# Four scans from kept last states, the third tile added by GpSimd in every step, and membrane and group statistics read from PSUM

## The reference, cut to what matters

```
xn = groupnorm(x)                          # 32 groups of 8 channels
xh, z = split(xn @ W_in)                   # 512 + 512 channels
xc = depthwise_conv_3x3(xh)
dt_r, B, C = split(xc @ W_xproj)           # 8, 16, 16
dt = softplus(dt_r @ W_dt + b_dt)
dtN = dt @ W_dtN + b_dtN
for t in range(2304):                      # per image, 512 channels d, 16 states n
    h[d,n] = exp(dt[t,d] * A[n]) * h[d,n] + dtN[t,n] * B[t,n] * xc[t,d]
    y[t,d] = sum_n h[d,n] * C[t,n] + Dskip[d] * xc[t,d]
x = x + (layernorm(y) * ln_g + ln_b) * silu(z) @ W_out + b_out

u = groupnorm(x) @ W.T + b                 # the 8 images are the 8 time steps
for t in range(8):
    v = v + (u[t] - v) / 2                 # membrane, one value for each pixel and channel
    s = v >= 1
    v = v * (1 - s)
    x[t] = x[t] + s
```

## Time and profile before

| | us |
|---|---|
| median of 3 runs | 4882.54 |
| the runs | 4874.4, 4884.55, 4882.54 |
| the profiled execution | 4875.24 |
| its span in the profile | 4873.4 |
| DVE, POOL, PE, ACT busy | 4382.4, 4151.5, 3694.4, 3122.2 |

### The profile page before, as it was taken

The page is one execution under the profiler, slowest core; times in us unless marked ns, Lnnn a source line. Parts: engine busy times, 40 slices in busy tenths (PEclk is TensorE's granted clock), DMA queues, the critical chain, the costliest instruction groups (busy, mean ns, idle before and its releaser), DMA issues.

```text
span 4873.4 us, 75732 instructions
## 1 busy us (share of the span) xinstructions
PE 3694.4 (76%) x20244; PEld 2332.2 (48%) x20244; DVE 4382.4 (90%) x4205; ACT 3122.2 (64%) x4578; POOL 4151.5 (85%) x3243
## 2 busy tenths in 40 slices
PE   4788787778777777777877777777777777877766
PEld 1455444545454544455544544445544554544443
DVE  0899999999999999999999999899989999999994
ACT  1677676666766676666766666666666666666662
POOL 1899999888988899888988889888888888998891
PEclk8889888988988899888888889998988898889986
DMA  2222212222222212222222212222221222122200
GB/s 56 85 65 74 66 58 65 77 69 63 62 69 67 76 47 78 60 77 60 65 63 73 64 57 78 67 60 60 80 71 50 60 84 67 59 63 70 68 32 20
DMA packets 189421, 315.36 MB, mean 65 GB/s; under 512 B 51992, under 2 KB 164120, under 8 KB 188960
## 3 DMA queue, kind: packets, MB, share of 16 engines
q1 hardware_dynamic: 188960, 310.06, 21.6%
HBM read 171.87 MB, written 20.05 MB: 39 GB/s over the span
## 4 chain that ended last, share of the span: by engine, by line
issue 30%; POOL 30%; DVE 18%; PE 15%; ACT 2%; SPq 2%; DVEq 1%; POOLq 1%; DMA 1%; ACTq 0%
POOL st L543 24%; DVE st L955 11%; PE ht L1088 5%; DVE y L932 3%; PE work L1061 2%; PE work L1154 2%; SPq L416 2%; POOL y L590 2%; POOL carry L567 1%; POOL st L550 1%; POOL xb L599 1%; PE work L1161 1%; PE work L1115 1%; PE work L1148 1%; PE work L1173 1%
## 5 line engine op out<-in xcount | busy, mean ns | idle before, releaser
L955 DVE TENSOR_TENSOR_SCAN st<-decay,st 128x1024 f32<-128x1024 f32 (+1 forms) x1536 | 2729.0, 1777 | 123.2 <-ACT decay L696 47.8
L543 POOL TENSOR_TENSOR st<-xc,bbc 128x1536 f32<-128x1536 f32 x768 | 2649.6, 3450 | 14.0 <-DMA bbc<-brow 11.1
L696 ACT ACTIVATE decay<-dt,neg_a 128x1024 f32<-128x1024 f32 (+1 forms) x1536 | 1360.1, 900 | 640.9 <-DVE st L955 634.3
L1088 PE MATMUL ht<-ident,st 128*128 128x128 f32 x9216 | 1414.2, 309 | 384.4 <-DVE st L955 382.2
L1088 PEld LDWEIGHTS ht<-ident,st 128*128 128x128 f32 x9216 | 1205.4, 159 | 683.9 <-issue 435.9
L932 DVE SCALAR_TENSOR_TENSOR y<-ht,ct,y 128x512 f32<-128x512 f32 x1536 | 1117.7, 728 | 129.2 <-PE ht L1088 126.6
L590 POOL TENSOR_TENSOR y<-y,weighed 128x512 f32<-128x512 f32 x624 | 792.6, 1270 | 276.0 <-ACT weighed L717 273.5
L717 ACT ACTIVATE weighed<-ht,ct 128x512 f32<-128x512 f32 x624 | 427.5, 685 | 438.6 <-PE ht L1088 436.0
L1061 PE MATMUL work<-tri,conv_w 96*32 96x384 f32 x4608 | 485.8, 561 | 130.6 <-issue 82.7
L1120 PE MATMUL work<-xn,win 128*128 128x384 f32 x768 | 318.6, 556 | 119.6 <-DVE ob L897 64.9
L1115 PE MATMUL work<-xn,win 128*128 128x480 f32 x768 | 359.2, 592 | 5.1 <-ACT xn L813 3.1
(11 more groups left out here) (93 smaller groups left out, 3870.8 us busy)
## 6 DMA issues: line engine op xcount, KB each, us to landing
bbc<-brow SPq DMA_DIRECT2D x192, 768.0 KB, 4.7
tri<-xhp SPq DMA_DIRECT2D x2304, 50.0 KB, 2.0
xin<-in_x_dram SPq DMA_DIRECT2D x48, 384.0 KB, 3.2
out_dram<-ot SPq DMA_DIRECT2D x48, 384.0 KB, 5.6
brow<-xp SPq DMA_DIRECT2D x48, 24.0 KB, 1.5
win<-in_L_conv_W_in_dram SPq DMA_DIRECT2D x1, 1024.0 KB
wo<-in_L_conv_W_out_dram SPq DMA_DIRECT2D x1, 512.0 KB
w1s<-in_L_conv_W_dram SPq DMA_DIRECT2D x1, 256.0 KB, 3.3
```

The costliest lines, as they stand in the source:

```text
L543: u = g.tensor_tensor(slot, xc[:, kq % 2, :, :], bbc[:, piece_slot(kq, p), n % PIECE, :].unsqueeze(1).to_broadcast([P, DC, T]), ALU.mult)
L696: a.activation(flat(decay[:, :, :])[:, lo:hi], flat(dt[:, (k + ahead) % 2, :, :])[:, lo:hi], ACT.Exp, scale=neg_a[:, n:n + 1]).then_inc(s_ ...
L955: v.tensor_tensor_scan(state[:, lo:hi], flat(decay[:, :, :])[:, lo:hi], state[:, lo:hi], 0.0 if h == 0 else state[:, lo - 1:lo], ALU.mult, ...
L1088: last = t.transpose(ht[:, m, c * P:(c + 1) * P], st[:, j, c, m * P:(m + 1) * P], ident[:, :])
```

## The change

It has these parts.

1. Scans: four for each step, one for each channel group of 384 columns. Each starts from the last state that is kept in `carry` (from the constant 0 in iteration 0). The first column's 1e30, `a0`, `cs`, POOL's small additions and the waits for them are gone. The last states are now copied by ACT, right after the decays of the next step (`save_carry`). The decays keep their two parts; scans 0 to 2 of a step come before the first addition to y, scan 3 before the second; scan 2 waits for the second decay part as well.
2. OWN is gone: ACT weighs and POOL adds the third tile in all 16 steps.
3. Membrane: DVE charges in place in PSUM (`charge_and_fire`: work + bias + volt, then the comparison with the threshold plus the image), for each half in its own step, between scan 3 and the second addition to y. ACT copies the charge from PSUM to `volt`, after its carry copy (`copy_membrane`). At the end of the step DVE resets from PSUM and the copy (`reset`), and only this frees the bank. So that the factor 0.5 needs no instruction, volt is kept in a unit that doubles from image to image (`units`, `b1cs`, and a factor in `w1s`).
4. Group statistics: the deviation from the mean and its square are read from and written to the PSUM bank, so that no instruction has two SBUF tensors; the bank is freed at the end.

```diff
-OWN = (8, 10, 11,)
-NWT = NS - len(OWN)
 CUT = 1024
-FAR = 1e30
-LEAST = 1e-28
+PARTS = ((0, CUT), (CUT, DC * T))
...
             def scan_input(b, k, n, ahead):
...
-                u = g.tensor_tensor(slot, xc[:, kq % 2, :, :],
-                                    bbc[:, piece_slot(kq, p), n % PIECE, :].unsqueeze(1).to_broadcast([P, DC, T]),
-                                    ALU.mult)
-                if kq > 0:
-                    u.then_inc(s_ux, 1)
-                    pool.wait_ge(s_ux, (bq * (K - 1) + kq - 1) * NS + n + 1)
-                    pool.wait_ge(s_cs, (bq * (K - 1) + kq - 1) * NCS + 1 + max(0, n - NCOPY + 1))
-                    g.tensor_tensor(st[:, j, :, 0], st[:, j, :, 0], cs[:, :, n], ALU.add).then_inc(s_u, 1)
-                else:
-                    u.then_inc(s_u, 1)
+                g.tensor_tensor(st[:, j, :, :], xc[:, kq % 2, :, :],
+                                bbc[:, piece_slot(kq, p), n % PIECE, :].unsqueeze(1).to_broadcast([P, DC, T]),
+                                ALU.mult).then_inc(s_u, 1)
...
             def accumulate_last(b, k, n, before):
...
-                if n in OWN:
-                    return
...
+                def save_carry(n, before):
+
+                    kq = (k - before) % K
+                    i = (b * K + k - before) * NS + n
+                    act.wait_ge(s_scan, i + 1)
+                    a.activation(carry[:, :, n], st[:, (kq * NS + n) % 3, :, T - 1], ACT.Copy).then_inc(s_carry, 1)
...
+                def copy_membrane(kc, h):
+
+                    act.wait_ge(s_spike, ((b - 1) * K + kc) * CH + h + 1)
+                    hold("act", act, b)
+                    i = turn(b, k, f"l{kc}_{h}")[0]
+                    a.activation(volt[:, h, kc * T:(kc + 1) * T], work[:, i, 0:T], ACT.Copy).then_inc(s_kept, 1)
...
                     next_decay(s)
+                    if main and k < K - 1:
+                        save_carry(s, 0)
+                    for kc, a0_step in (L1_SLOTS.get(k, ()) if L1 in do else ()):
+                        if s in (a0_step, a0_step + 1):
+                            copy_membrane(kc, s - a0_step)
...
-                v.tensor_copy(gn_mu[w][:, :], work[:, i, 0:CH]).then_inc(emptied[i], 1)
...
+                mean, off, square = (work[:, i, j * CH:(j + 1) * CH] for j in range(3))
+                v.tensor_copy(gn_mu[w][:, :], mean)
+                v.tensor_tensor(gn_dm[w][:, :], gn_mv[w][:, :, 0], mean, ALU.subtract).then_inc(s_gdv[w], 1)
+                v.tensor_tensor(off, gn_mv[w][:, :, 0], mean, ALU.subtract).then_inc(s_gdv[w], 1)
...
-                v.scalar_tensor_tensor(out=volt[:, :, cols], in0=ob[:, :, :], scalar=0.5,
-                                       in1=volt[:, :, cols], op0=ALU.mult, op1=ALU.add).then_inc(s_volt, 1)
...
+                now = work[:, i, 0:T]
+                v.scalar_tensor_tensor(out=now, in0=now, scalar=b1s[:, h:h + 1], in1=volt[:, h, cols],
+                                       op0=ALU.add, op1=ALU.add).then_inc(s_volt, 1)
+                dve.wait_ge(s_volt, il + 1)
+                hold("dve", dve, b)
+                v.scalar_tensor_tensor(out=ob[:, h, :], in0=now, scalar=units[:, 1:2],
+                                       in1=img[:, img_par(b, -1), h, cols], op0=ALU.is_ge,
+                                       op1=ALU.add).then_inc(s_spike, 1)
+
+            def reset(b, k, kc, h):
...
+                dve.wait_ge(s_kept, ((b - 1) * K + kc) * CH + h + 1)
+                hold("dve", dve, b)
+                i = turn(b, k, f"l{kc}_{h}")[0]
+                now = work[:, i, 0:T]
+                v.scalar_tensor_tensor(out=volt[:, h, cols], in0=now, scalar=units[:, 1:2], in1=volt[:, h, cols],
+                                       op0=ALU.is_lt, op1=ALU.mult).then_inc(emptied[i], 1)
...
-            def scan(b, k, n, h):
+            def scan(b, k, n, c):
...
+                if c == 0:
                     dve.wait_ge(s_u, i + 1)
+                    if k > 0:
+                        dve.wait_ge(s_carry, (b * (K - 1) + k - 1) * NS + n + 1)
+                    dve.wait_ge(s_dec[0], i + 1)
+                if c == 2:
+                    dve.wait_ge(s_dec[1], i + 1)
+                state = st[:, (k * NS + n) % 3, c, :]
+                last = v.tensor_tensor_scan(state, decay[:, c, :], state, carry[:, c, n:n + 1] if k > 0 else 0.0,
+                                            ALU.mult, ALU.add)
+                if c >= 2:
+                    last.then_inc((s_scan0, s_scan)[c - 2], 1)
```

More of the change, by code:

```diff
@@ L339, in flat @@
             return v.rearrange("p c t -> p (c t)")
-        def weighings(q, n):
-            return q * NWT + sum(m not in OWN for m in range(n))
         def img_par(b, d=0):
@@ L588, in accumulate_last @@
                     pool.wait_ge(s_y2, i)
-                pool.wait_ge(s_wt, weighings(b * K + k - before, n + 1))
+                pool.wait_ge(s_wt, i + 1)
                 g.tensor_tensor(y[:, kq % 2, NTD, :], y[:, kq % 2, NTD, :], weighed[:, n % 2, :],
@@ L718, in weigh @@
                                  scale=ct[:, kq % 2, NTD * NS + n:NTD * NS + n + 1]).then_inc(s_wt, 1)
-                def first_decay():
-                    e = b * (K - 1) + k
-                    act.wait_ge(s_dt, q1 + 1)
-                    need(act, s_cs, e * NCS)
-                    if isinstance(b, int) and b <= 0:
-                        act.wait_ge(s_set_dve, 3)
-                    for c in range(DC):
-                        last = a.activation(a0[:, c, :], neg_a[:, :], ACT.Exp, scale=dt[:, p1, c, 0:1])
-                    last.then_inc(s_a0, 1)
                 def exp_and_log():
@@ L896, in half_charge @@
                 i = await_filled(dve, b, k, f"l{kc}_{h}")
-                v.scalar_tensor_tensor(out=ob[:, h, :], in0=work[:, i, 0:T], scalar=b1s[:, h:h + 1],
-                                       in1=volt[:, h, cols], op0=ALU.add, op1=ALU.subtract).then_inc(emptied[i], 1)
-            def charge(b, k, kc):
-                cols = slice(kc * T, (kc + 1) * T)
-                for h in range(CH):
-                    await_emptied(dve, b, k, f"l{kc}_{h}")
-                v.scalar_tensor_tensor(out=volt[:, :, cols], in0=ob[:, :, :], scalar=0.5,
-                                       in1=volt[:, :, cols], op0=ALU.mult, op1=ALU.add).then_inc(s_volt, 1)
@@ L967, in iteration @@
                         if main:
-                            scan(b, k, s, h)
+                            for c in ((0, 1, 2), (3,))[h]:
+                                scan(b, k, s, c)
+                        if h == 1 and L1 in do:
+                            for kc, a in L1_SLOTS.get(k, ()):
+                                if s in (a, a + 1):
+                                    charge_and_fire(b, k, kc, s - a)
                         if s >= Y_LAG and main:
@@ L1007, in iteration @@
                             if s in (a, a + 1):
-                                half_charge(b, k, kc, s - a)
-                            if s == a + 1:
-                                charge(b, k, kc)
-                            if s == a + 2:
-                                fire(b, k, kc)
+                                reset(b, k, kc, s - a)
                     if TIN in do and k in TIN_CHUNKS and s - 1 in TIN_STEPS:
@@ L1035, in iteration @@
                             jw = await_filled(dve, b, k, "b1")
-                            v.tensor_tensor(b1s[:, :], work[:, jw, 0:CH], b1c[:, :], ALU.add).then_inc(emptied[jw], 1)
+                            dve.wait_ge(s_w1s, b)
+                            v.scalar_tensor_tensor(out=b1s[:, :], in0=work[:, jw, 0:CH], scalar=units[:, 0:1],
+                                                   in1=b1cs[:, :], op0=ALU.mult, op1=ALU.add).then_inc(emptied[jw], 1)
             walk(dve, iteration)
@@ L1081, in transposes @@
                         else:
[L1082 to L1086 removed]
+                            need(pe, s_wt, i)
                         for c in range(DC):
```

123 lines of the change are left out of this document (26 added, 97 removed).

## The result

The changed kernel takes 5010.42 us in the median of 4 runs (4999.72 to 5012.27) against 4881.06 for the kernel before: ratio 1.0262, 95% interval [1.0244, 1.0281], 129 us slower. I had forecast 4950 and slower; the way was right, the rise is not the 70 of that forecast but 129. 5010 lies inside the whole range (4815 to 5030) and just above the 4900 to 5000 of my own case. The profiled executions took 4875.24 and 5012.27, 137 apart; what is read from traces adds up to that, and not to 129.

The account below looks back on a forecast made before the run. POOL was taken to bound steps 8 to 14, DVE steps 14 to 8. +10.7 and -4.4 made +6.3 us an image, +44 for seven; first image +24, tail +2: +70, 4945, stated as 4950; range 4815 to 5030.

Parts of the forecast that it names:

- my own case: The prediction's main case for the whole kernel: 4950 us, 4900 to 5000, chance 0.44.
- the bound it rested on: Steps 8 to 14: POOL is the bound there, busy 32.06 of 33.50 us, and the added additions lengthen them.
- Without a chunk: Steps 8 to 14 without membrane work: +3.1 us, scan 11 starting 1.8 later, at 18.9 after step 8.
- With a chunk at step 9 in iteration 1: Steps 8 to 14: the reset waits for ACT's copy, scan 10 at 13.7, scan 11 at 20.4; +0.9 us.
- The first image: The image without membrane work: 6 x 3.1 us in steps 8 to 14 and some 6 more, +24.
- Iterations 2, 3 and 4 in these steps: Steps 8 to 14: +1.5 us each in iterations 2 and 3 (0.9 to 2.3), +0.6 in 4 (0 to 1).
- Steps 14 to 8: The rest of an image: -4.4 us; -1.4 each in iterations 2 to 4, -2.2 in 1, after 1.7 given back.
- -6.1 + 3.0: Steps 14 to 8, iterations 2 to 4: shorter membrane chunk saves 6.1 us, ten steps with longer scans add 3.0.
- Prices of instructions: DVE: four scans at 0.92 us each (0.87 in the first iteration), new membrane instructions 0.61 (0.53 without overlap).
- ledger -84: DVE's total work: +204 scans, -95 third tile's addition, -160 membrane, -33 group statistics, -84 us.
- The third rival: Scans at the upper bound (+40 us) with iterations 2 and 3 copy stalls at 2.3 (+11): 5000 us, chance 0.12.
- the whole 0.3: DVE's scans: two more a step cost 0.3 us by the row, against 0.12 by the skill's 58 cycles.

Follow-up runs that it names:

- e2: The kernel before with part 2 alone (OWN empty, POOL also adds the third tile for n = 8, 10, 11): 4964.18 us, ratio 1.0152.
- e4: The changed kernel with OWN = (8, 10, 11) back, DVE adding the third tile there, so parts 1, 3 and 4: 4886.1 us, ratio 0.9980.
- e8: The changed kernel with DVE instead of ACT copying the membrane charge in step 9: 4960.66 us, ratio 1.0153, 50 us under the changed kernel.
- e1: The kernel before with parts 3 and 4 alone (membrane and group statistics from PSUM), two scans and OWN kept: 4824.4 us, ratio 0.9874.
- e6: The changed kernel with the third tap's convolution rows left out, 8 DMAs for each channel group instead of 12: 4835.26 us, ratio 0.9888.
- e3: The kernel before with part 1 alone (four scans from kept last states, OWN and old membrane stay): 4978.33 us, ratio 1.0184.

## Why the prediction was right or wrong

**The direction, and the bound it rested on: right.** Steps 8 to 14 cost +14.8 us an image (242.7 against 227.9), and e2 and e4 put all of it on part 2. Without a chunk I had worked out +3.1 us, 36.6 in iteration 5; measured 36.70 there, and 36.39 in iteration 0 (+2.6). Scan 11 at 18.9 us after step 8: 19.0. With a chunk at step 9 in iteration 1, 40.7: 40.89 on the mean, 40.39 in the fourth image, with scan 10 at 13.55 and scan 11 at 20.62 after step 8 (worked out: 13.7 and 20.4). The reset at step 9 waits for ACT as foreseen (e8: 50 us). The first image: +24 forecast, +27.4 measured, but that sum is partly luck: steps 8 to 14 brought 14.1 and not 18.6, the rest 13.3 and not 6.

**Iterations 2, 3 and 4 in these steps: mis-sized.** I bounded 2 and 3 by 0.9 and 2.3 and took 1.5; they cost 2.96 and 2.84, above my upper bound. For iteration 4 I took 0.6; it cost 2.0. Together 4.2 us an image, 25 us in the six images of the table. In iterations 2 and 3 DVE idles 3.05 and 2.9 us in step 9, 1.92 of it before the reset, against 1.9 and 1.65 in iteration 1. Iteration 4 has no chunk at step 9; there scan 11 waits 1.9 us for POOL, as in iterations 0 and 5 (2.2).

**Steps 14 to 8: the step that failed most.** I wrote that the membrane saves 6.1 us in each of iterations 2 to 4 and that "about 1.7 of the gain is given back" to the convolution rows, -4.4 us an image in all. Measured: +1.4 (362.9 against 361.5), 5.8 us an image and 35 in the six images. With the 25 of above this is 60 of the 67 us by which the profiled execution is over the forecast. Iteration 1's stretch fell by 5.7 as against my 2.2; those of 2, 3 and 4 rose by 0.8, 1.1 and 1.8 where I had -1.4.

In e1, without the longer scans, some 24 us less DVE work an image brought 4.8 in the rest. The membrane's saving itself came: DVE's work in the stretch from iteration 1 to 2 fell by 3.25 us (61.26 to 58.01), as -6.1 + 3.0 said. But DVE's idle time in steps 0 to 7 of iterations 2 to 4 rose from 0.5 to 4.8 us, and I had allowed 1.7 for it. e6 shows what it is: with fewer rows that idle time falls to 1.8 and the rest of an image by 19.7.

The traces show why it is so much. Iteration 2 of the fourth image, first the issue of the rows, then the first and the last convolution group; the kernel before:

```profile
2059.95 15.29 SPq L416 DMA_DIRECT2D tri<-xhp  x24
2057.68 2.14 PE L1061 MATMUL work<-tri,conv_w 96*32 96x384 f32 x24
2081.67 2.14 PE L1061 MATMUL work<-tri,conv_w 96*32 96x384 f32 x24
```

The changed kernel:

```profile
2124.23 16.05 SPq L404 DMA_DIRECT2D tri<-xhp  x24
2121.95 2.14 PE L1000 MATMUL work<-tri,conv_w 96*32 96x384 f32 x24
2141.70 3.84 PE L1000 MATMUL work<-tri,conv_w 96*32 96x384 f32 x24 [3.42 <-issue]
```

Counted from scan 0 of the iteration (2043.67 and 2104.31), the first group (cv0, in step 2) went from 14.0 to 17.6. Step 2 now starts at 14.6 and not at 12.1, since DVE's charge, comparison and reset of the first half stand in step 1, and the transposes and the membrane's product still come ahead of cv0 on PE. The last group follows the first by 24.0 us in the kernel before, where nothing holds it, and by 19.8 in the changed kernel, where it waits for the rows; so it comes at 38.0 and 37.4. DVE reached step 6 3.6 us earlier than before and gained nothing by it. I had named this late comer and its place, and priced it from one iteration without a chunk, where DVE's wait is 3.67, without asking when cv0 starts in the iterations that have one.

**Prices of instructions: right.** Scans 0.92 and 0.86 (taken 0.92 and 0.87); membrane 0.60 to 0.62 (taken 0.61); DVE's busy time -105 (ledger -84). The third rival's number (5000) is nearer than mine, but its first half, dearer scans, didn't come; its second, the stalls of iterations 2 and 3, did. The one mechanism of the change that does what it says is the membrane's: L905 took 0.96 to 3.71 us and L913 0.96 to 4.04, while the 288 instructions with one operand in PSUM that came in their place all took 0.60 to 0.63. The traces agree here with the Trainium skill (SBUF — State Buffer, "Who interferes with whom"): with a single SBUF input the instruction no longer waits for GpSimd.

Four scans cost 0.28 us more than two with a kept start value (4 x 0.917 against 2.199 + 1.191 from start to start), and 0.04 more with a constant (4 x 0.857). So a start value from memory costs 0.06; the old second scan had one, the new four have four, which makes 0.18 of the 0.28, and what is left for two more instructions is 0.10. For that part the Trainium skill (VectorE: DVE Perf Modes, "The TRN2 errata", 58 cycles with SBUF operands) gives 0.12, an estimate, and the trace nearly agrees; the page's row for a PSUM source, where the scans' decay lies, has 120 cycles, which would be 0.25, and doesn't fit. In the prediction I set the page's figure against the whole 0.3: I hadn't taken the start values apart.

**How the parts add.** By the medians e1, e2 and e3 make -67, +73 and +87, 93 together, where the changed kernel has +129; by their ratios 103 against 128, and the intervals, of 0.2% to 0.25% each, almost cover the gap. By the table they make -6.7, +9.8 and +12.8 us an image, 15.9 together against 16.3. So on the whole the parts add, as far as these runs can tell. By stretch they don't: in steps 8 to 14 they make -2.0, +14.9 and +16.8 against +14.8, in the rest -4.8, -5.2 and -4.1 against +1.4. That fits the one hold which e6 shows in the rest, the convolution rows: gains that come one by one don't come together. No run tests it. The price of part 2 changes in the same way, 73 us alone and 124 on top of the other parts (by the medians of the changed kernel and e4; 138 by their ratios): 15 us an image in steps 8 to 14 both times, but in the rest e2 gained 5.2 and the changed kernel nothing.

The scans depend on what stands beside them. On top of the new membrane they cost 62 us by the medians of e4 and e1 (52 by their ratios), not 87; in steps 8 to 14, 1.8 us an image (e4 over e1) and not 16.8 (e3 over before). The traces say why, from the distances of DVE's starts in these steps. The scans took 8.3 us more in both. In e4 DVE's idle time fell by 6.2. In e3 the old instructions with two SBUF operands became longer, though nobody changed them: L913 and L916 (there L848 and L851) went from 1.1 and 1.7 us to 3.1 and 2.5, and with the group statistics this makes 11 us an image. That is the conflict with POOL, moved here by the change of times, while L913's mean over the whole kernel fell.

## What to carry to other kernels

When two engines are near saturation, find the stretch in which each of them is the bound before moving work between them: here 144 instructions of 1.3 us, moved to the engine with the smaller total into the very steps where it had no slack, cost 73 us in the kernel before and 124 to 138 in the changed one. Work taken off the busiest engine counts only up to the next chain that arrives late; here two thirds of 195 us were lost in e1, the larger part in the steps that wait for DMAs issued one by one, and a one-line move of their trigger was worth 48 us. And price such a late comer in each kind of iteration, not in the one where it can be seen already.

## What the runs showed of the hardware

The conflict of DVE with POOL isn't a fixed price: in the kernel before the 48 instructions of L913 took between 0.96 and 4.04 us, and L913, unchanged, had a mean of 2412 ns in the kernel before, 1370 in e2 and 1845 in e3 (there L848), as other work shifted it against POOL's instructions (the shift is inferred, since the edits leave these instructions as they were); L916 went from 1299 to 949 and 1756. The same scan form is 0.06 us cheaper with a constant start value than with one from memory (938 against 1000 ns). SyncE took 0.64 us to issue each copy of 50 KB, and each landed 2.0 us after its issue in the median, with a third fewer of them too.
